# Two flamingo layers on one core: the row stage gets three orders of its blocks on each engine, and scaling and final sum one round sooner

## What is computed

```python
def reference(x, ctx_2048, mask_BxS2_if0, g_xattn, g_ffn, ...):
    x = x + jnp.tanh(g_xattn[0]) * _L0_xattn_ref(_layernorm(x, axis=-1), ctx_2048, w_qkv, w_proj, b_proj)
    x = x + jnp.tanh(g_ffn[0]) * _L0_ffn_ref(_layernorm(x, axis=-1), weight, bias)
    x = x + jnp.tanh(g_xattn[1]) * _L1_xattn_ref(_layernorm(x, axis=-1), ctx_2048, mask, W_in, b_in, g_res, g_init)
    x = x + jnp.tanh(g_ffn[1]) * _L1_ffn_ref(_layernorm(x, axis=-1), rhs)
    return x
...
def _L0_ffn_ref(x, weight, bias):
    i_scale = jnp.max(jnp.abs(x)) / 127.0          # one scale for the whole tensor
    q_input = jnp.clip(jnp.round(x / i_scale), -128.0, 127.0)
...
def _L1_xattn_ref(...):                             # rmsnorm, product with W_in, plus a gathered recurrence
    h = jnp.einsum('bld,ed->ble', rmsnorm(embeds, g_res), W_in) + b_in
...
def _L1_ffn_ref(lhs, rhs):
    lhs_scale = jnp.max(jnp.abs(lhs), axis=2, keepdims=True) / 127.0    # one scale per row
    q_lhs = jnp.round(lhs / lhs_scale)
    return (q_lhs @ q_rhs) * lhs_scale * rhs_scale
```

## The kernel before

| step | due | what and where |
|---|---|---|
| live(n) | 0 | ACT L1467: first normalisation of a block, scaled for rounding (2 instructions) |
| ROUND0 | 1 | POOL L1220: rounding |
| TRQ | 2 | PE L1257 (ms_ps, identb): transposes; ACT L1437: copy to `qqT` |
| MM0 | 2 | PE L1263, L1266 into misc: ternary product with bias |
| UPD0 | 3 | DVE L1373: x + product; L1397, L1414: statistics of the new rows (bn_stats, bn_aggr) |
| STAT0, STAT1 | 3, 6 | POOL L1231 to L1238: five small instructions for both statistics at once, "STAT" below |
| NORM1 | 4 | ACT L1451: normalisation (2 instructions) |
| LOAD | 4 | SP L1189, L1190: two loads for the recurrence |
| TRX | 5 | PE L1257 (pv_ps, ident): transposes; ACT L1432: copy to `yxT` |
| MM1 | 5 | PE L1301, L1303: product in f32, with the recurrence |
| UPD1 | 6 | DVE L1368: x + product; L1392, L1407: statistics |
| NORM3 | 7 | ACT L1459: normalisation (2 instructions) |
| AMAX | 8 | DVE L1379: largest magnitude per row; POOL L1216: scale `ls3` from it |
| QUANT | 8 | DVE L1401: reciprocal of the scale; L1419: multiply and round (2 instructions) |
| TR3 | 9 | PE L1257 (ms_ps, identb): transposes; ACT L1443: copy to `q3T` |
| MM2 | 10 | PE L1263 into aux or st_ps: last product |
| SCALED | 11 | DVE L1386: product times both scales, into `prod` (2 instructions) |
| FINAL | 12 | POOL L1210: x + prod, into `outb` (2 instructions); SP L1194: output transfer |

## Time and profile before

### The profile page before, as it was taken

The page is one execution under the profiler, slowest core; times in us unless marked ns, Lnnn a source line. Parts: engine busy times, 40 slices in busy tenths (PEclk is TensorE's granted clock), DMA queues, the critical chain, the costliest instruction groups (busy, mean ns, idle before and its releaser), DMA issues. The chain is left out here.

```text
span 1077.5 us, 26415 instructions
## 1 busy us (share of the span) xinstructions
PE 1034.7 (96%) x8627; PEld 706.9 (66%) x8627; DVE 873.9 (81%) x2219; ACT 795.2 (74%) x1731; POOL 696.4 (65%) x1347
## 2 busy tenths in 40 slices
PE   5999999999999999999999999999999998999994
PEld 3466666666666666666666666666666555888872
DVE  8767888888887788888888887888887866899996
ACT  3377777777777777777777777777777755999983
POOL 5566666666666666666666666666666314588876
PEclk9999999999999999999999999999999999999996
DMA  7855555666655555555556555655545311133332
GB/s 152 132 104 107 107 108 111 114 113 107 109 108 108 107 109 112 110 111 109 108 110 112 111 112 111 110 110 109 100 98 93 68 29 38 61 101 114 100 111 89
DMA packets 140908, 111.31 MB, mean 103 GB/s; under 512 B 15650, under 2 KB 136932, under 8 KB 140772
## 3 DMA queue, kind: packets, MB, share of 16 engines
q1 hardware_dynamic: 140185, 109.16, 50.0%
q10 hardware_dynamic: 587, 0.47, 0.2%
HBM read 30.33 MB, written 16.32 MB: 43 GB/s over the span
## 5 line engine op out<-in xcount | busy, mean ns | idle before, releaser
L980 DVE TENSOR_REDUCE neg<-ms_ps 128x1 f32<-128x376 f32 x1024 | 525.9, 544 | 155.9 <-PE ms_ps L733 150.4
L1069 ACT ACTIVATE probs<-st_ps 128x512 f32<-128x512 f32 x768 | 442.4, 603 | 23.5 <-PE st_ps L723 22.8
L733 PE MATMUL ms_ps<-qk 96*128 96x376 bf16 x1024 | 332.8, 325 | 3.1 <-DVE neg L980 2.5
L723 PE MATMUL st_ps<-qk 99*128 99x256 bf16 x1536 | 294.4, 273 | 0.9 <-DMA qk<-negT 0.6
L723 PEld LDWEIGHTS st_ps<-qk 99*128 99x128 bf16 x1536 | 133.6, 98 | 125.1 <-issue 40.3
L748 PE MATMUL pv_ps<-probs,v 128*32 128x256 f32 (+1 forms) x3072 | 194.4, 383 | 0.0
L771 PE MATMUL misc<-xnT,wqkvT 128*128 128x256 f32 x512 | 152.3, 382 | 2.0 <-DVE wqkvT L862 1.3
L733 PEld LDWEIGHTS ms_ps<-qk 96*128 96x128 bf16 x1024 | 98.4, 96 | 70.3 <-DVE neg L980 50.2
L748 PEld LDWEIGHTS pv_ps<-probs,v 128*32 128x32 f32 (+1 forms) x3072 | 96.1, 110 | 55.8 <-ACT probs L1069 12.7
L565 POOL TENSOR_SCALAR parts<-qk 128x632 bf16<-128x632 f32 x63 | 45.4, 721 | 125.5 <-ACT qk L1142 125.5
L1076 ACT COPY negT<-aux 24x256 bf16<-24x256 bf16 x64 | 22.9, 357 | 102.2 <-PE aux L789 102.2
(11 more groups left out here) (205 smaller groups left out, 1761.9 us busy)
## 6 DMA issues: line engine op xcount, KB each, us to landing
qk<-parts SPq DMA_DIRECT2D x254, 94.0 KB, 3.6
qk<-parts SPq DMA_DIRECT2D x128, 158.0 KB, 3.7
qk<-parts SPq DMA_DIRECT2D x256, 64.0 KB, 3.5
out_dram<-xn SPq DMA_DIRECT2D x32, 256.0 KB, 2.3
xs<-in_x SPq DMA_DIRECT2D x31, 256.0 KB, 2.9
cx<-in_ctx SPq DMA_DIRECT2D x32, 240.0 KB, 4.0
recurrence_input<-u_in SPq DMA_DIRECT2D x32, 120.0 KB, 2.8
plug<-plugs SPq DMA_DIRECT2D x32, 120.0 KB, 3.4
```

The source lines that it names most:

```text
L723: mm = pe.matmul(st_ps[u % SR][:, j * S:(j + 1) * S], k6[0:KM, r, h, k * P:(k + 1) * P], q6[0:KM, r, h, :], start=True, stop=True)
L733: pe.matmul(ms_ps[t][:, 0:KEYS], q6[0:KR, r, h % HU, t * P:(t + 1) * P], k6[0:KR, r, h % HU, 0:KEYS], start=True, stop=True).then_inc(s_ms, 1)
L980: dve.tensor_reduce(neg[:, m, t, h % HU:h % HU + 1], ms_ps[t][:, 0:KEYS], AX.X, ALU.max, negate=True).then_inc(s_red, 1)
L1069: act.activation(probs[:, u % PR, :], st_ps[u % SR][:, :], ACT.Exp).then_inc(s_exp, 1)
```

## The change

`SCALED` goes from 11 to 10 and `FINAL` from 12 to 11, so there are 43 rounds and not 44. Each engine's `body` becomes three functions: `ramp` for rounds 0 to 6, `body` for 7 to 37 (`TAIL` = 38) and `last` from there. The pieces are the same instructions with the same waits; their order in a round is:

| engine | before, all rounds | ramp | body | last |
|---|---|---|---|---|
| SP | LOAD, FINAL | same | same | same |
| POOL | FINAL, AMAX, ROUND0, STAT | AMAX, FINAL, ROUND0, STAT | AMAX, ROUND0, FINAL, STAT | FINAL, STAT, ROUND0, AMAX |
| PE | TRX, TRQ, TR3, MM2, MM1, MM0 | TRQ, MM2, TR3, TRX, MM0, MM1 | as before | TRQ, MM2, MM0, MM1, TRX, TR3 |
| ACT | TRX, TRQ, TR3, NORM1, NORM3, live(n) | NORM3, TR3, TRQ, TRX, live(n), NORM1 | TRX, TRQ, NORM3, NORM1, TR3, live(n) | TR3, live(n), NORM1, TRX, NORM3, TRQ |
| DVE | UPD1, UPD0, AMAX, SCALED, stats 1, stats 0, reciprocal, aggr 1, aggr 0, QUANT | UPD0, reciprocal, stats 0, aggr 0, AMAX, UPD1, QUANT, stats 1, aggr 1, SCALED | AMAX, UPD1, UPD0, stats 1, stats 0, aggr 1, reciprocal, aggr 0, QUANT, SCALED | UPD0, stats 0, AMAX, UPD1, aggr 0, stats 1, aggr 1, SCALED, reciprocal, QUANT |

The diff, cut to the constants and to the order of the pieces; the pieces' other lines are as before:

```diff
@@ -1168,12 +1168,15 @@
         ROUND0, MM0, UPD0, STAT0, NORM1, MM1, UPD1, STAT1 = 1, 2, 3, 3, 4, 5, 6, 6
-        NORM3, AMAX, QUANT, MM2, SCALED, FINAL, LOAD, TRQ, TRX, TR3 = 7, 8, 8, 10, 11, 12, 4, 2, 5, 9
-
-        def rounds(body):
+        NORM3, AMAX, QUANT, MM2, SCALED, FINAL, LOAD, TRQ, TRX, TR3 = 7, 8, 8, 10, 10, 11, 4, 2, 5, 9
+
+        RAMP = 7
+        TAIL = NB + 6
+
+        def rounds(ramp, body, last):
 
             for n in range(NB + FINAL):
-                body(n)
+                (ramp if n < RAMP else body if n < TAIL else last)(n)
 
...
         def pool_rows(pool):
...
+            def body(n):
+                if live(n - AMAX):
...
+                    pool.tensor_scalar(ls3[:, B % 4, :], am3[:, 0, :], 1e-12, 1.0 / 127.0, ALU.max, ALU.mult).then_inc(r_ls, 1)
+                if live(n - ROUND0):
...
+                    pool.tensor_scalar(yq[q], yq[q], 1.0, ROUND + FP16_1536, ALU.mult, ALU.add).then_inc(r_q, 1)
+                if live(n - FINAL):
+                    B, q = n - FINAL, (n - FINAL) % 2
+                    pool.wait_ge(r_p, (B + 1) * T)
...
+                        pool.tensor_tensor(outb[:, q, t, :], xs[:, B, t, :], prod[q][:, t, :], ALU.add).then_inc(r_out, 1)
+                if live(n - STAT0) or live(n - STAT1):
...
+            def last(n):
+                if live(n - FINAL):
...
+                if live(n - STAT0) or live(n - STAT1):
...
+                if live(n - ROUND0):
...
+                if live(n - AMAX):
...
+            rounds(ramp, body, last)
...
         def tensor_rows(pe):
...
+            def ramp(n):
+                if live(n - TRQ):
...
+                if live(n - TRX):
...
+                if live(n - MM0):
...
+                if live(n - MM1):
...
+            def last(n):
+                if live(n - TRQ):
...
+                if live(n - MM2):
...
+                if live(n - TRX):
...
+                if live(n - TR3):
...
             def body(n):
+                if live(n - AMAX):
...
+                    dve.tensor_reduce(am3[:, 0, :], y3[q], AX.X, ALU.max, apply_absolute_value=True).then_inc(r_am, 1)
                 if live(n - UPD1):
...
+                if live(n - UPD1):
...
+                        dve.bn_stats(bn1[:, t, :], xs[:, B, t, :]).then_inc(r_x3, 1)
+                if live(n - UPD0):
...
+                        dve.bn_stats(bn[:, t, :], xs[:, B, t, :]).then_inc(r_x2, 1)
+                if live(n - UPD1):
...
+                        dve.bn_aggr(mv23[:, 1, t, :], bn1[:, t, :]).then_inc(r_x3, 1)
+                if live(n - QUANT):
...
+                    dve.reciprocal(am3[:, 1, :], ls3[:, B % 4, :]).then_inc(r_rc, 1)
+                if live(n - UPD0):
...
+                if live(n - QUANT):
...
+                    ins.then_inc(r_q3, 1)
+                if live(n - SCALED):
+                    B, q = n - SCALED, (n - SCALED) % 2
+                    dve.wait_ge(r_m2, B + 1)
+                    if live(B - 2):
+                        dve.wait_ge(r_out, (B - 1) * T)
+                    for t in range(T):
+                        dve.scalar_tensor_tensor(prod[q][:, t, :], m2_ps[q][:, t * C:(t + 1) * C], ls3[:, B % 4, t:t + 1],
+                                                 w1s[:, :], ALU.mult, ALU.mult).then_inc(r_p, 1)
...
+            def last(n):
+                if live(n - UPD0):
...
                 if live(n - AMAX):
...
-                if live(n - SCALED):
-                    B, q = n - SCALED, (n - SCALED) % 2
-                    dve.wait_ge(r_m2, B + 1)
-                    if live(B - 2):
-                        dve.wait_ge(r_out, (B - 1) * T)
-                    for t in range(T):
-                        dve.scalar_tensor_tensor(prod[q][:, t, :], m2_ps[q][:, t * C:(t + 1) * C], ls3[:, B % 4, t:t + 1],
-                                                 w1s[:, :], ALU.mult, ALU.mult).then_inc(r_p, 1)
...
+                if live(n - SCALED):
...
+                if live(n - QUANT):
...
         def scalar_rows(act):
...
             def body(n):
                 if live(n - TRX):
...
+                if live(n - NORM3):
...
+                if live(n - NORM1):
...
                 if live(n - TR3):
...
+                if live(n):
...
```

More of the change, by code:

```diff
@@ L1313, in body @@
                     product(misc, qqT, w0T, r_m0, bias_r)
-            rounds(body)
+            def last(n):
+                if live(n - TRQ):
+                    B, q = n - TRQ, (n - TRQ) % 2
+                    pe.wait_ge(r_q, B + 1)
+                    wait(pe, r_cq, B)
+                    transposes(tq_ps[:, :].bitcast(BF16), yq_low[q], identb, r_tq)
+                    if n < MM1:
+                        busy(pe, 3, wide=True)
+                if live(n - MM2):
+                    B, q = n - MM2, (n - MM2) % 2
+                    pe.wait_ge(r_c3, B + 1)
+                    if live(B - 2):
+                        pe.wait_ge(r_p, (B - 1) * T)
+                    product(m2_ps[q], q3T, w1q, r_m2)
+                if live(n - MM0):
+                    B = n - MM0
+                    pe.wait_ge(r_cq, B + 1)
+                    if live(B - 1):
+                        pe.wait_ge(r_x2, (B - 1) * 5 + 1)
+                    if B == 0:
+                        pe.wait_ge(r_bias, 11)
+                    product(misc, qqT, w0T, r_m0, bias_r)
+                if live(n - MM1):
+                    B, q = n - MM1, (n - MM1) % 2
+                    pe.wait_ge(r_cx, B + 1)
+                    if live(B - 2):
+                        pe.wait_ge(r_x3, (B - 2) * 5 + 1)
+                    pe.wait_ge(d_in[q], (B // 2 + 1) * 32)
+                    for t in range(T):
+                        for k in range(KT):
+                            pe.matmul(m1_ps[q][:, t * C:(t + 1) * C], yxT[:, k, t * P:(t + 1) * P], winT[:, k, :],
+                                      start=(k == 0), stop=False)
+                        mm = pe.matmul(m1_ps[q][:, t * C:(t + 1) * C], gath[0:NP + 1, q, t * P:(t + 1) * P],
+                                       u_in[0:NP + 1, q, :], start=False, stop=True)
+                    mm.then_inc(r_m1, 1)
+                if live(n - TRX):
+                    B, q = n - TRX, (n - TRX) % 2
+                    pe.wait_ge(r_yx, (B + 1) * T)
+                    wait(pe, r_cx, B)
+                    transposes(pv_ps, yx[q], ident, r_tx)
+                if live(n - TR3):
+                    B, q = n - TR3, (n - TR3) % 2
+                    pe.wait_ge(r_q3, B + 1)
+                    wait(pe, r_c3, B)
+                    transposes(t3_ps[:, :].bitcast(BF16), y3_low[q], identb, r_t3)
@@ L1438, in body @@
                                    bias=cst[:, 1:2]).then_inc(r_cq, 1)
[L1439 to L1444, removed]
+                if live(n - NORM3):
+                    B, q = n - NORM3, (n - NORM3) % 2
+                    act.wait_ge(r_n, (B + STAT1 - STAT0 + 1) * 5)
+                    if live(B - 2):
+                        act.wait_ge(r_t3, B - 1)
+                    for t in range(T):
+                        act.activation(y3[q][:, t, :], xs[:, B, t, :], ACT.Identity, bias=rn23[:, 1, 1, t:t + 1],
+                                       scale=rn23[:, 0, 1, t:t + 1]).then_inc(r_y3, 1)
                 if live(n - NORM1):
@@ L1452, in body @@
                                        scale=rn23[:, 0, 0, t:t + 1]).then_inc(r_yx, 1)
+                if live(n - TR3):
+                    B = n - TR3
+                    act.wait_ge(r_t3, B + 1)
+                    wait(act, r_m2, B)
+                    act.activation(q3T, t3_ps[:, :].bitcast(FP16)[:, 0:KT * S].rearrange("p (k r) -> p k r", k=KT), ACT.Identity,
+                                   bias=cst[:, 1:2]).then_inc(r_c3, 1)
+                if live(n):
+                    B, q = n, n % 2
+                    if live(B - 2):
+                        act.wait_ge(r_tq, B - 1)
+                    for t in range(T):
+                        c = B * T + t
+                        act.activation(yq[q][:, t, :], xs[:, B, t, :], ACT.Identity, bias=nm1[:, c:c + 1],
+                                       scale=am1[:, c:c + 1]).then_inc(r_y, 1)
```

333 lines of the change are left out of this document (305 added, 28 removed).

## The result

The changed kernel takes 1074.53 us (median of 6 runs, 1073.75 to 1076.64), the kernel before 1081.05 beside it (6 runs, 1079.57 to 1082.04): ratio 0.9948, 95% interval 0.9937 to 0.9959. The forecast was 1078.5 with a range from 1075.5 to 1081.8.

What follows compares the result with a forecast made beforehand. DVE was taken to bound the middle, with fill and drain each having its own limit. Drain gains of 2.1 + 0.9 = 3.0 us off 1079.27 gave 1076.3; adding 2.3 for the median gave 1078.5, range 1075.5 to 1081.8.

Steps and rivals of the forecast that it cites:

- the clock in the fill: Fill, round 5: TensorE's clock still falls and returns at about 907, so MM1 ends at 908.7 instead of 908.46.
- the way from the profiled execution to the median: Whole kernel: the median of three runs was taken as 2.3 us higher than the profiled execution.
- Rival 1: Fill: the clock does not fall in round 5, 1.4 us more gained, 1077.1; chance 0.15.
- The middle: Rounds 11 to 34: DVE-bound with the same instructions, so the pitch stays 4.84 us a round.
- the 0.4 that I worked out: Middle rounds: FINAL ends at 3.19 of a round and QUANT stands at 3.56, 0.4 us of room.
- The drain: Last rounds: STAT every 3.64 instead of 4.12, 2.1 us gained, plus 0.9 from the last TR3 copy.
- The gain is one round of the drain: Due rounds: SCALED and FINAL one round sooner save one drain round; no separate size given.
- The slower one (2): Middle: QUANT and FINAL meet in every round, 23 rounds by 0.36, 1086.8; chance 0.09.
- Rival 3: Drain collisions in 35 to 38 fall on the path, or the fill ends unchanged: 1.2 gained, 1080.3; chance 0.22.
- Rival 4: Whole kernel: the order changes nothing and the saved round was already covered by POOL, 1081.5; chance 0.06.

Runs made afterwards that it cites:

- e1_due: The kernel before with only the due rounds changed (SCALED 10, FINAL 11), old order in all rounds: 1080.71 us, ratio 1.0002.
- b2: The kernel before, unchanged, timed and profiled once more: 1081.05 us, ratio 1.0001.
- e2_order: The changed kernel with the old due rounds (SCALED 11, FINAL 12), so the three orders alone: 1077.19 us, ratio 0.9968.
- a2: The changed kernel, unchanged, timed and profiled once more: 1075.94 us, ratio 0.9956.
- e8_warm: The changed kernel with GpSimd in the middle's order in the last rounds and 23 filler matmuls in TensorE's gaps of the last four: 1074.57 us, ratio 0.9933.
- e9_ramp12: e8_warm with the first order kept until round 11 on TensorE and ScalarE: 1087.38 us, ratio 1.0056.
- e4_filler: The kernel before with six filler matmuls in TensorE's wait at the head of round 5: 1079.59 us, ratio 0.9996.
- e10_inplace: e8_warm with the last five final sums written into the rows themselves and stored from there: 1072.41 us, ratio 0.9928.
- e6_meet: The changed kernel with reciprocal and quantisation moved ahead of the first update's statistics in DVE's middle order: 1091.96 us, ratio 1.01.
- e3_old_ramp: The changed kernel with the old order in rounds 0 to 6 on every engine: 1077.88 us, ratio 0.9968.

## Why the prediction fell short

Two steps failed: the clock in the fill (1.4 of the stage), and the way from the profiled execution to the median (the larger part). The forecast was 1078.5 and the median is 1074.53, 4.0 less. The stage was 1.6 shorter than forecast (179.3 for 180.9), it began 1.9 later in the profiled execution (895.50 for 893.57), and the median lies 2.1 below that execution (1076.64), where I had it 2.3 above, a swing of 4.4: 1.6 - 1.9 + 4.4 is the 4.0 but for rounding.

**The fill: the first failed step is the clock.** "If the clock comes back when it does now (about 907)" was the assumption; the clock never fell. Rival 1, with a chance of 0.15, priced that at 1.4 us, and it is what happened. In stage time: MM1 of round 5 was forecast to end at 908.7 - 893.57 = 15.1 and ended at 909.11 - 895.50 = 13.6; AMAX of round 11 was forecast at 931.0 - 893.57 = 37.4, or 36.0 by rival 1, and came at 931.28 - 895.50 = 35.8. I held it against the rival that TensorE's idle stretch shrinks only from 1.56 to 1.05; it did shrink to 1.02. That was an argument from one trace. e1_due and b2 show that even 1.55 and 1.56 lead to no fall in one run and a long one in another: one trace could not give the chance. With nine traces of nine without a fall, 0.15 was too low.

**The middle: right.** Forecast pitch 4.84, measured 4.85 with DVE at 20.00 of 20. The first quantisation and final sum met in round 11 (1.10 for 0.59, so 0.5 where I had 0.36); in round 12 the sum ran 0.17 into the quantisation, which took 0.59 all the same, where I had 0.15. That the two errors cancel is luck. The room between final sum and quantisation is the 0.4 that I worked out.

**The drain: right, but for tenths.** Forecast in stage time against measured: STAT of 34 153.1 and 151.65, STAT of 35 157.5 and 156.0, STAT of 37 164.8 and 163.5, AMAX of 39 170.0 and 168.7. Each is 1.3 to 1.5 sooner, which is the clock of the fill carried along. STAT came every 3.75, not 3.64: the sum of GpSimd's pieces left 0.1 out. The last copy follows its transposes as forecast. The end was 0.2 better still: in the kernel before, the last final sum began 2.94 after the last copy, waiting for its output buffer's DMA at the end, and now it begins 2.76 after it, waiting for the scaling alone; I had carried what follows the copy over unchanged.

**The due rounds.** "The gain is one round of the drain" had no price of its own and is not what the runs show: by themselves the due rounds cost 1.1 (e1_due), and on top of the orders they bring 0.9 (e2_order), the wait for an output buffer.

**The sum.** Forecast 3.0 off a stage of 183.9; measured 4.6, that is 3.0, 1.4 for the clock, and 0.2. Of the 4.6, 1.2 is the fall that the first trace of the kernel before happened to have; against that kernel at full clock the change brings 3.4 (182.7 and 179.3).

**From the profile to the median: the second failed step.** I added 2.3 to come from the profiled execution to the median of three runs, as if the distance were a constant. It is a spread with causes. One is the clock in round 5, which cost 0, 1.2 or 3.0 us. The profiled execution of the kernel before took 1079.27 and had a fall of 1.2; that of b2, the same kernel, took 1081.21 and had one of 3.0. Of the 1.9 between them 1.8 is in the stage. So the 2.3 was in all likelihood mostly a longer fall, which the new order didn't show in any trace, and I carried it over.

The other is where the row stage starts. Over all traces that is 893.0 to 895.7. In the five traces where the granted clock of the first 50 us is 0.93 (after, a2, e2_order, e8_warm, e9_ramp12) it is 894.1 to 895.7, in the three where it is 1.00 (e1_due, e4_filler, e10_inplace) 893.0 to 893.6; at 0.97 there are starts of 893.4 and of 895.2, so this is not the whole of it. Nor is it shown that the start is independent of the edit, as the expectation of a2 has it: the four traces with one order for all rounds start at 893.1 to 893.7, and eight of the ten with three functions at 894.1 or later, though nothing ahead of the stage differs. Two traces of one kernel differ by 0.1 (before, b2) and by 1.0 (after, a2).

At full clock the two stages differ by 3.4; the medians differ by 4.8 to 6.5. The rest, 1.4 to 3.1, is of the size of the two falls seen, 1.2 and 3.0, but e4_filler, which has the old orders without the fall, lies only 1.2 under the kernel before. So up to 1.9 of it stays unexplained. The range, to 1075.5, had only the spread of three runs under rival 1.

**The rivals.** The slower one (2) didn't come about; e6_meet shows that its price is real. Rival 3 was wrong: of the collisions it feared, the new one (1.05 in round 36) was hidden, since STAT followed GpSimd's own work there, and the two on the last chain (1.33 and 1.58) stood in the kernel before too. I had collisions of up to 1.0 in each of rounds 35 to 37; in 35 and 37 the quantisation took 0.62. Rival 4 is refuted by the interval, which ends at 0.9959.

## What to carry to other kernels

A fill is limited by what its first blocks wait for, a middle by its busiest engine, and a drain by one chain: an order for each can pay (here the first did, while the third brought nothing over the middle's), but each order holds good only as long as the blocks that it puts first have nothing to wait for (e9_ramp12). A step moved a round sooner gains nothing by itself when it then waits at the head of a queue (e1_due). A wait removed is worth less than its length when it had kept two engines apart that hinder each other (e10_inplace), or when the next one is as long (e8_warm). And a clock level seen in one trace is one draw: look at a second trace before a sum is built on it.

## What was not expected of the hardware

- The same instructions with the same wait of 1.55 to 1.56 us ahead of them ran at full clock in one trace, and fell from 2.4 to 1.2 GHz in three (before, b2, e3_old_ramp), for stretches that cost 1.2 to 3.0 us. In e9_ramp12 waits of 2.35 and 2.62 were followed by the low clock, waits of 1.95 and 2.31 by the high one.
- A pair of DVE quantisations beside two GpSimd additions took 1.05 to 1.66 where it takes 0.59 alone, and the additions grew from 1.42 to 1.46 (1.50 in e10_inplace). Where they overlapped by less than 0.2 (rounds 12, 35 and 37 of the changed kernel), the pair took 0.59 to 0.62. The Trainium skill (SBUF — State Buffer, Who interferes with whom) says that the two engines exclude each other for such forms; the runs agree, and show nearly all of the cost on VectorE.
- The row stage began anywhere within 2.7 us over the 14 traces, with the same instructions ahead of it; within one kernel the two traces differ by up to 1.0.
